# Head mixing of a two-layer kernel moved behind the per-head products: regrouped through off-chip memory and mixed by ten TensorE products instead of 80 GpSimd multiplications

## What is computed

```
q, k, v = split_heads(x @ Wq), split_heads(x @ Wk), split_heads(x @ Wv)   # 16 memory keys and values ahead of k and v
dots = einsum('bhid,bhjd->bhij', q, k) * d ** -0.5
dots = einsum('bhij,hk->bkij', dots, pre_proj)       # heads mixed before the softmax
...                                                   # causal mask, the 64 largest of a row kept, softmax
attn = einsum('bhij,hk->bkij', attn, post_proj)      # and behind it
out = einsum('bhij,bhjd->bhid', attn, v) ... @ Wo + bo
```

## Time and profile before

| | us |
|---|---|
| median of three runs (1109.30 to 1110.75) | 1109.37 |
| the profiled execution | 1110.47 |
| its span in the profile | 1108.8 |
| busy: PE 958.9, DVE 887.2, ACT 746.1, POOL 554.5 | |

### The profile page before, as it was taken

How to read it: one execution, slowest core, us unless ns; L and a number is a source line. 1 busy time by engine, 2 the same in 40 slices (tenths; PEclk the granted TensorE clock), 3 DMA queues, 4 the chain that set the end, 5 groups by cost and what they waited for, 6 DMA issues and landing times.

```text
span 1108.8 us, 16210 instructions
## 1 busy us (share of the span) xinstructions
PE 958.9 (86%) x4177; PEld 595.4 (54%) x4177; DVE 887.2 (80%) x2862; ACT 746.1 (67%) x1947; POOL 554.5 (50%) x1183
## 2 busy tenths in 40 slices
PE   8749678769999898999998999978989777999998
PEld 4234335426666666666666666655656555533333
DVE  5958687549999998999998999988999994354444
ACT  5022112369999998999998999977999793412221
POOL 5907551026767775767666676754666561000000
PEclk9968889889999999999999999989999998799999
DMA  7000000000000000000000000000000000000000
GB/s 233 1 0 1 0 0 1 1 0 2 1 2 2 2 1 1 1 2 1 2 2 1 2 1 2 2 1 1 2 1 2 1 2 1 1 0 10 9 10 10
DMA packets 5533, 8.81 MB, mean 8 GB/s; under 512 B 1632, under 2 KB 3232, under 8 KB 5280
## 3 DMA queue, kind: packets, MB, share of 16 engines
q1 hardware_dynamic: 5408, 7.51, 2.0%
HBM read 6.46 MB, written 1.05 MB: 7 GB/s over the span
## 4 chain that ended last, share of the span: by engine, by line
DVE 53%; PE 25%; issue 10%; ACT 7%; POOL 2%; DVEq 1%; POOLq 1%; ACTq 1%; DMA 0%
DVE Ex L863 11%; DVE top L814 7%; DVE mixed L808 6%; DVE Sx L777 4%; DVE unread L795 3%; DVE yk L886 2%; PE bA L462 2%; PE bBC L462 2%; DVE away L802 2%; PE bBC L463 2%; PE bH L481 2%; PE bFGI L481 2%; PE bFGI L463 2%; PE bFGI L386 2%; ACT unread L584 1%
## 5 line engine op out<-in xcount | busy, mean ns | idle before, releaser
L1073 POOL TENSOR_TENSOR mixed<-Sx,nthr 128x528 f32<-128x528 f32 (+3 forms) x256 | 185.5, 757 | 11.6 <-issue 11.6
L386 PEld LDWEIGHTS bFGI<-spread,Ex 128*128 128x128 f32 x1280 | 155.1, 199 | 65.4 <-POOL spread L1092 63.3
L400 PE MATMUL bH<-turned 128*128 128x512 f32 (+3 forms) x512 | 153.1, 442 | 36.6 <-ACT turned L611 36.3
L386 PE MATMUL bFGI<-spread,Ex 128*128 128x128 f32 x1280 | 164.9, 286 | 22.1 <-POOL spread L1092 22.0
L584 ACT ACTIVATE unread<-Sx,nthr 128x144 bf16<-128x144 f32 (+3 forms) x256 | 144.0, 564 | 23.8 <-POOL nthr L1054 19.8
L400 PEld LDWEIGHTS bH<-turned 128*128 128x128 f32 x512 | 92.0, 189 | 97.0 <-issue 76.7
L592 ACT ACTIVATE unread<-Sx,nthr 128x144 bf16<-128x144 f32 (+3 forms) x256 | 143.4, 566 | 0.0
L863 DVE SCALAR_TENSOR_TENSOR Ex<-mixed,yk,Ex 128x144 f32<-128x144 f32 (+3 forms) x256 | 139.1, 596 | 1.7 <-ACT Ex L603 1.0
L603 ACT ACTIVATE Ex<-Sx,nmax 128x144 f32<-128x144 f32 (+3 forms) x256 | 125.5, 563 | 0.0
L814 DVE MAX8 top<-mixed 128x8 f32<-128x528 f32 (+3 forms) x256 | 110.8, 493 | 0.0
L1092 POOL TENSOR_TENSOR spread<-ident,rinv 128x512 f32<-128x512 f32 x64 | 66.6, 1041 | 87.5 <-DVE rinv L866 87.5
(11 more groups left out here) (282 smaller groups left out, 1886.7 us busy)
## 6 DMA issues: line engine op xcount, KB each, us to landing
xr<-in_xT SPq DMA_DIRECT2D x4, 256.0 KB, 3.6
w_s<-in_w12T SPq DMA_DIRECT2D x1, 1024.0 KB, 6.4
outT<-xc SPq DMA_DIRECT2D x4, 256.0 KB, 2.0
wq_s<-in_WqT SPq DMA_DIRECT2D x1, 512.0 KB, 3.9
wk_s<-in_WkT SPq DMA_DIRECT2D x1, 512.0 KB, 4.4
wv_s<-in_WvT SPq DMA_DIRECT2D x1, 512.0 KB, 4.3
wo_s<-in_Wo SPq DMA_DIRECT2D x1, 512.0 KB, 4.7
w_s<-in_w3T SPq DMA_DIRECT2D x1, 512.0 KB, 6.9
```

The lines of the kernel that those rows point to most:

```text
L386: last = mm(bFGI[:, k * P:k * P + P], Ex[g % 2][:, t, a:a + P], spread[:, t, :], start=True, stop=True)
L400: last = mm(bH[:, jt * P:T], u[:, jt, :], PT[:, at:at + n], start=h + jt == 0, stop=False)
L1073: Gp.tensor_tensor(y[ph][t], Sx[ph][:, t, 0:NT[t]], nthr[ph][1][:, t:t + 1].broadcast_to((P, NT[t])), ALU.add).then_inc(sem("y_ready"), 1)
```

## The change

- `head_products(i)` makes, for i = 0 (keys) and 1 (values), 16 products of one head each (64 rows, 128 columns) and 16 small ones (16 columns) for the memory part. ScalarE's `head_copies(i)` writes them into `per_head[i]`, 128 partitions x 16 heads x 144 columns, in six copies.
- SP stores `per_head[i]` to a tensor in off-chip memory (1.18 MB) and reads it back so that a partition holds one head of one of eight groups of 16 rows: eight transfers of 16x16 pieces of 576 bytes (144 values), into `turned_heads[i]`, which shares `mixed` with the buffers of the loop over heads.
- `mix` is now one product of 128x512 (the fifth of each i 128x256) with the block-diagonal matrix `spread_heads[i]`, eight copies of `pre` or `post` that SP loads after GpSimd has zeroed the matrix. ScalarE copies the result back into `turned_heads[i]`. There are ten such jobs; after the fifth of each i SP stores the result and reads it back regrouped into `per_head[i]`, of which `AT`, `G` and `Bw` are now views.
- The eleventh job turns the memory part of i = 1 into `Um`: GpSimd gathers it in one copy (`um_turned`), PE transposes it twice, ScalarE copies it.
- The 80 multiplications on GpSimd are gone, and with them the broadcast loads of `pre` and `post`.
- In the loop over heads one instruction on 128x4 values gets a second bit operation (`TWO`).

The core of the diff:

```
@@ @@
 def mix_jobs():
-    return iter(range(10))
+    for i in range(2):
+        for lo in range(0, PAIRS, 512):
+            yield i, lo, min(PAIRS, lo + 512)
+    yield 2, 0, 2 * D
...
+            "w_mix": [(spread_heads[i][H * k:H * k + H, H * k:H * k + H], w) for i, w in enumerate((pre, post)) for k in range(PART)],
...
+            for i in range(2):
+                sp.wait_ge(sem("heads_copied"), 6 * i + 6)
+                sp.dma_start(heads_store[i], per_head[i][:, :, :].rearrange("p h n -> p (h n)")).then_inc(sem(f"heads_stored{i}"), 16)
+            for i in range(2):
+                sp.wait_ge(sem(f"heads_stored{i}"), 16)
+                for k in range(PART):
+                    rows = slice(H * k, H * k + H)
+                    sp.dma_start(turned_heads[i][rows, :].rearrange("p (s n) -> p s n", n=HD),
+                                 heads_store[i][rows, :].rearrange("s (h n) -> h s n", n=HD)).then_inc(sem(f"heads_turned{i}"), 16)
...
-            mix(3)
+            head_products(0)
+            head_products(1)
+            pe.wait_ge(sem("heads_copied"), 12)
...
-            mix(1)
+            mix(2)
...
                 if b < 2:
-                    mix(1)
+                    mix(2 - b)
...
                 if b < B - 1:
                     gate_up(b + 1)
-                    mix(1)
+                if b < 2:
+                    mix(2)
...
             deviations(2)
-            pe.wait_ge(sem("mix_copied"), 10)
+            mix(1)
+            pe.wait_ge(sem("mix_copied"), 11)
+            pe.wait_ge(sem("mix_back0"), 16 * PART)
...
-                V.tensor_scalar(flips[:, :], away[:, :].bitcast(I32), REST, None, ALU.bitwise_or).then_inc(sem("flips_ready"), 1)
+                V.tensor_scalar(flips[:, :], away[:, :].bitcast(I32), REST, TWO, ALU.bitwise_or, ALU.bitwise_xor).then_inc(sem("flips_ready"), 1)
...
-            for j in mix_jobs():
-                if j == 0:
-                    for key in ("w_qk", "w_vo"):
-                        pool.wait_ge(sem(key), LOADED[key])
-                for c in range(C):
-                    if j:
-                        pool.wait_ge(sem("mix_used"), C * (j - 1) + c + 1)
...
-                        last = Gp.tensor_tensor(mixed[:, c, :, :], w[:, c, :].unsqueeze(1).broadcast_to((P, 4, D)),
-                                         heads.unsqueeze(2).broadcast_to((P, 4, D)), ALU.mult)
...
-            pool.wait_ge(sem("mix_copied"), 10)
+            for i in range(2):
+                pool.wait_ge(sem(f"mix_back{i}"), 16 * PART)
+            Gp.tensor_copy(um_turned[:, :, :], UmT).then_inc(sem("um_gathered"), 1)
```

More of the change, by code:

```diff
@@ L18 @@
 C = H * DH // P
+HD = D + MEM
+PART = P // H
+PAIRS = P // PART * HD
 NE, RH, SH = 8, 128, 4
@@ L222, in _, with head_products @@
         def _(pe):
-            jobs = mix_jobs()
+            jobs = enumerate(mix_jobs())
+            def head_products(i):
+                pe.wait_ge(sem(("w_qk", "w_vo")[i]), LOADED[("w_qk", "w_vo")[i]])
+                left, right, kept = ((wk_s, wq_s, mk_s), (wv_s, wo_s, mv_s))[i]
+                for k in range(2):
+                    if i:
+                        pe.wait_ge(sem("heads_copied"), 6 if k == 0 else 2 * k + 2)
+                    for j in range(4):
+                        for half in range(2):
+                            rows = slice(DH * half, DH * half + DH)
+                            last = mm(octo[4 + 2 * half + k][:, j * D:j * D + D], left[rows, 4 * k + j, :], right[rows, 4 * k + j, :], start=True, stop=True)
+                            if j == 3:
+                                last.then_inc(sem(f"heads_done{half}"), 1)
+                pe.wait_ge(sem("heads_copied"), 6 * i + 2)
+                for c in range(C):
+                    for half in range(2):
+                        rows = slice(DH * half, DH * half + DH)
+                        last = mm(octo[4 + 2 * half][:, c * MEM:c * MEM + MEM], right[rows, c, :], kept[rows, c, :], start=True, stop=True)
+                        if c == C - 1:
+                            last.then_inc(sem(f"heads_done{half}"), 1)
@@ L244, in mix @@
-                    pe.drain().then_inc(sem("mix_done"), 1)
+                    j, (i, lo, hi) = next(jobs)
+                    pe.wait_ge(sem("mix_copied" if j else "w_mix"), j if j else LOADED["w_mix"])
+                    if i == 2:
+                        pe.wait_ge(sem("um_gathered"), 1)
+                        for a in range(2):
+                            last = nc.tensor.transpose(bH[:, a * P:a * P + P], um_turned[:, 8 * a:8 * a + 8, :], ident[:, :])
+                    else:
+                        if lo == 0:
+                            pe.wait_ge(sem(f"heads_turned{i}"), 16 * PART)
+                        last = mm(bH[:, 0:hi - lo], spread_heads[i][:, :], turned_heads[i][:, lo:hi], start=True, stop=True)
@@ L246, in means @@
+                    last.then_inc(sem("mix_done"), 1)
             def means(q, sequences):
@@ L487, in _, with head_copies @@
             cp = ACT.Copy
-            jobs = mix_jobs()
+            jobs = enumerate(mix_jobs())
+            def head_copies(i):
+                for k in range(2):
+                    for half in range(2):
+                        act.wait_ge(sem(f"heads_done{half}"), 3 * i + k + 1)
+                        nc.scalar.activation(per_head[i][:, 8 * k + half:8 * k + 8:2, 0:D], octo[4 + 2 * half + k].rearrange("p (h d) -> p h d", h=4), cp).then_inc(sem("heads_copied"), 1)
+                for half in range(2):
+                    act.wait_ge(sem(f"heads_done{half}"), 3 * i + 3)
+                    nc.scalar.activation(per_head[i][:, half:H:2, D:HD], octo[4 + 2 * half][:, 0:C * MEM].rearrange("p (h m) -> p h m", h=C), cp).then_inc(sem("heads_copied"), 1)
             def mix_copy(k=1):
                 for _ in range(k):
-                    j = next(jobs)
+                    j, (i, lo, hi) = next(jobs)
                     act.wait_ge(sem("mix_done"), j + 1)
[L494 to L500, removed]
+                    if i == 0:
+                        last = nc.scalar.activation(turned_heads[0][:, lo:hi], bH[:, 0:hi - lo], cp, scale=float(DH) ** -0.5)
+                    elif i == 1:
+                        last = nc.scalar.activation(turned_heads[1][:, lo:hi], bH[:, 0:hi - lo], cp)
                     else:
@@ L992, in _ @@
             Gp = nc.gpsimd
+            for w in spread_heads:
+                last = Gp.memset(w[:, :], 0.0)
+            last.then_inc(sem("heads_zeroed"), 1)
             Gp.memset(ident[:, :], 0.0)
```

75 lines of the change are left out of this document (31 added, 44 removed).

## The result

The changed kernel takes **1131.32 us** (median of four, 1130.23 to 1133.08) against 1109.34 before (median of four). The ratio is 1.0209 with a 95% interval from 1.0182 to 1.0235: it is slower by about 22 us (the interval leaves out 1), where 1074.2 had been forecast. The profiled execution took 1130.47, with a span of 1128.7.

The account below looks back on a forecast made before the run. VectorE was taken to bound the first 227 us, its instructions lengthened by GpSimd's multiplications beside them. Gains of 36.8 less 0.5 (Um) and 1.1 (clock) gave 35.2 us, so a median of 1074.2 us, range 1068 to 1083.

Parts of the forecast that it names:

- Rival D: VectorE's steps stay long because something other than GpSimd's multiplications lengthens them; 1110 us, no change; chance 2%.
- Scans: From 21.75 to 35.05 us, four scans and four L726 lose GpSimd's company: gain 5.4, plus 0.4 at the start, 5.8 us.
- Weights: Quantising the weights, 35.05 to 66.75 us, falls from 31.70 to 19.0 us without GpSimd beside it: gain 12.7 us.
- Activations: Four activation `quantise` stretches, 88.72 to 125.09 us, fall from 36.37 to 23.8 us: gain 12.6 us.
- Feed-forward: The first three of four feed-forward stretches lose 3.4, 1.4 and 0.9 us against 11.71: gain 5.7 us.
- Products per head: PE's added products end at about 44.6 us, before VectorE's last weight at 48.3: cover 3.7 us, cost 0.
- rival A: TensorE becomes the bound before the product with C, if a product costs over 0.30 us; 1081 to 1092 us; chance 8%.
- Transfers: Storing and regrouping heads through off-chip memory, SP issuing at 0.43 us each, arrives before PE asks: cost 0, thinnest cover 16 us.
- Rivals B and C: Regrouped heads come late, for instance 1088 us, chance 5% (B); a regrouping runs on one engine, about 1300 us, chance 4% (C).
- Um: Two transposes and a copy between third layer norm and loop over heads: 1.4 instead of 0.87 us, cost 0.5 us.
- Clock: Lost TensorE filler costs 2.3 us at four products, less rest before the product with C gives back up to 2.4: net -1.1.
- step on the loop over heads: Loop over heads keeps its instructions, cost 0; rounding may shift the rare further-search branch by one, about 5 us; chance 1%.

Follow-up runs that it names:

- run with idle multiplications: Changed kernel with the tie-proof choice, plus 32 GpSimd multiplications of 128x512 whose result nobody reads; 1093.75 us (one run).
- tie-proof version: Changed kernel with the choice of the row's element made so that an even count also gives a position; 1073.05 us, ratio to before 0.9664.
- single round: Changed kernel with the full search cut from eight rounds to one; 1094.1 us (one run).
- both rounded: Query side's scale multiplied by 1 + 2^-20: on the kernel before, with TWO, 1136.55 us; on the changed kernel 1102.41 us (one run each).
- other GAIN: Changed kernel with GAIN = 0.701 in place of 0.7, moving every row's last threshold a little; 1100.61 us (one run).

## Why the prediction was wrong, point by point

- **The quantity to count** (0.68 us per instruction beside a GpSimd multiplication) was right, and the run with idle multiplications shows it directly. The Trainium skill, "SBUF — State Buffer", section "SBUF: two separate sides", says that a VectorE instruction with two SBUF inputs and a GpSimd one that reads SBUF exclude each other, the later one waiting; the 1.46 and 0.73 us of L726 with and without company agree. Rival D had no part.
- **Scans**: 5.8 forecast. They start 1.15 us earlier and take 6.2 less, 7.3. A scan alone takes 1.22 and in company 2.06 us: it lost 0.84 and not 0.68. The earlier start, forecast as 0.4, was 1.15. The loss of some 0.8 us that the prediction worked out from the Trainium skill, "DVE: opcode table, instruction layouts, handler registers and perf-mode slots", section 6, was nearer than mine by rows; for the scan alone its estimate of 1.1 us stands against 1.22 measured.
- **Weights**: 12.7 forecast, 12.2 measured (31.70 to 19.47). **Activations**: 12.6 forecast, 13.3 measured; a second lengthened step in the stretch that I took for clean was left out (L677 at 119.85, 0.43 us for 0.18). **Feed-forward**: 5.7 and 5.7.
- **Products per head**: 0 forecast and 0 measured, with far more cover than 3.7 us. In PE's timeline the products of two heads run at the same time:

```profile
22.20 0.37 PE L261 MATMUL bE<-wq_s,wk_s 64*128 64x128 f32 x1
22.20 0.37 PE L261 MATMUL bFGI<-wq_s,wk_s 64*128 64x128 f32 x1
```

  16 products take 2.05 us in all (22.20 to 24.25), 0.13 us each and not 0.24: two at a time, one on rows 0 to 63 and one on rows 64 to 127. The reason for "I take 0" did not hold, though: in the second sixteen, from 27.11 on, the granted clock fell to the lower level with PE at work all the time (columns of the earlier trace rows):

```profile
27.55:30.50 2.95, 2.95 (x34) 2.95 (x30) 2.08 (x8) 1.08 (x2) 0.00 (x0) 0.50 0.97 398
```

  They took 3.45 us, 0.22 each, still under the 0.30 at which rival A decides. PE was through at about 36 and waited 12.14 us for VectorE. Rival A had no part, thanks to the pairs and not to the clock.
- **Transfers**: 0 and 0. The 16 transfers of the first two regroupings were issued from 33.33 on, in SP's timeline, at 0.86 us each on average, twice the price I took. The way back, in pieces of the same 16x16x576 bytes, was issued at 0.47 each:

```profile
33.33 13.75 SPq L231 DMA_DIRECT2D mixed<-heads_store  x16
...
85.85 3.74 SPq L239 DMA_DIRECT2D per_head<-mixed_store  x8
```

  So it is not the shape of the transfer that costs 0.86; why the first sixteen were slow is open (twice as many were queued behind one another). The traffic ended by about 58, and PE's first mixing product at 68.20 waited for nothing. GpSimd's gathering copy came at 155.31, some 33 us ahead of its reader:

```profile
155.31 0.40 POOL L1072 COPY um_turned<-per_head 128x256 f32<-128x256 f32 x1 [147.53 <-DMA per_head<-mixed_store]
```

  Rivals B and C had no part; in the stretch from 40 to 60 us the mean share of all 16 engines was 1.03, so the regrouping did not fall to one.
- **Um**: 0.5 forecast, 0 measured. From the layer norm's last product to the first of the loop it is 0.87 us, as before: transposes and copy fit beside `xn`.
- **Clock**: -1.1 forecast. The loss came where it was put, at sequence 2's products (1.54 for the first pair at 130.74 where the earlier trace rows has 0.86 at 170.01; the way between the stretches grew from 4.85 to 7.29, 2.4 us). The gain was 1.4 in the second layer norm, not at the product with C, which still took 2.05: PE had rested 12.14 us ahead of it and not about 4, because the products per head were short. Net -1.0; that this is so near to -1.1 is partly luck.
- Together 7.3 + 12.2 + 1.4 + 13.3 + 5.7 - 2.4 and 0.3 in the ways between are the 37.8 us of the first part. The forecast of 1074.2 is the time of the tie-proof version, 1073.05, in which the same edits are timed without the two searches.
- **The step that failed** is the one on the loop over heads: "Same instructions" and "the rare branch that searches further could be taken once more or less than the three times here; it costs about 5 us", at 1%. I had the right cause, the other rounding, but read the price from the three events in the trace. They were all of the cheap kind, for which about 5 us is right. Inside that branch is a second one, whose price no row of before shows: 27.3 us in head 29 and 28.7 in head 63. Two of them outweigh the 37.8 us. The sum of known parts gave no room for it, so the range didn't hold the time, and the sign was wrong; the 5% for "slower" stood for late transfers alone, and the 1% for "same" did not even hold rival D's 2%. Whether the edited kernel comes out 36 us faster (as the tie-proof version does) or 22 us slower is luck of the rounding and no property of the new order of the work.

What is shown and what is argued: that the loss is two full searches is shown by the trace, by the single round and by their absence; that even counts cause them, by the tie-proof choice, which differs from the old one for even counts alone; that rounding decides who has them, by three kernels in which a change of a millionth in the scores or of about a thousandth in a threshold's step brought, removed or moved them. That the sign of an exact equality is what makes a count even is argued from the parity; no row shows the value. That the lengthening by company is the gain is shown for the scans and the weights and argued for the rest. How often a search happens is open: of the six kernels with different roundings or thresholds and the old choice that stand here (before, changed, both rounded, other GAIN, and TWO alone, which rounds as before), the numbers are 0, 2, 1, 1, 1 and 0.

## What to carry to other kernels

Where a kernel has branches on data, the arithmetic ahead of them is part of their price: before reordering it, read the code of every branch that the trace does not show, down to the innermost, and work out its cost even if it has not run. When a total comes out far from the sum, cut the span at the edge of the edited part first; here one look at one product told that the edit had gained all it should. And a full search, by the argument above an exact tie between a value and a threshold, is no unlikely event over 64 heads of 512 rows each: four of the six kernels had one. A choice that allows for it was free here and took 58 us off the changed kernel.

## What was not expected of the hardware

- Two products of 64 rows each, one on partitions 0 to 63 and one on 64 to 127, ran at the same time without being asked to: 0.13 us per product of 128 columns.
- A scan loses 0.84 us beside a GpSimd multiplication, where VectorE's other lengthened instructions on 512 columns lose 0.67 to 0.78 and TENSOR_REDUCE loses nothing (0.41 us on 256 columns both ways).
- Sixteen transfers of 16x16 pieces of 576 bytes took SP 0.86 us each to issue, and later ones of the same shape 0.47; plain loads took 0.43.
- In the software loop of the search, VectorE's instructions of 0.56 to 0.58 us leave a gap of about 1.1 us per round (0.98 in the tile of 528 columns).
- The same 2.74 us of filler brought the higher clock to sequence 2's products and not to sequence 3's, where PE rested 1 us longer behind it.
- The granted clock fell to 0.50 at about 27.5 us in the changed kernel while PE was busy, 0.4 us after a rest of 0.62 us.
